# Score runs of two query tiles on four PSUM banks, AV in a transposes' bank, and 256-column units for V, O and the plain FFN

## What is computed

```python
def attn(x, wq, wk, wv, wo):              # 16 heads of 64, window 256, x [16, 2048, 1024] float32
    ...                                   # q, k, v in blocks of 256 tokens, the block before in front of k and v
    scores = jnp.einsum('bhjqd,bhjkd->bhjqk', q, k2) / jnp.sqrt(Dh)
    band = (ki >= qi + 1) & (ki <= qi + W)
    ...
    attn = jax.nn.softmax(jnp.where(mask, scores, neg), axis=-1)
    out = jnp.einsum('bhjqk,bhjkd->bhjqd', attn, v2)
    return out.transpose(0, 2, 3, 1, 4).reshape(B, S, D) @ wo.T

def ffn(x, theta, phi, theta_noise, phi_noise):
    real = x @ jnp.cos(theta + theta_noise)
    imag = x @ jnp.sin(phi + phi_noise)
    return jnp.sqrt(real * real + imag * imag)

x = x + layernorm(attn(layernorm(x), wq, wk, wv, wo))
x = x + layernorm(ffn(layernorm(x), theta, phi, theta_noise, phi_noise))
```

## Time and profile before

| | |
|---|---|
| time, median of 3 runs | 2562.8 us (2562.77 to 2563.14) |
| the profiled execution's own time | 2564.06 us |
| its span, slowest core (2) | 2562.4 us |
| spans of the 8 cores | 2556.4 to 2562.4 us |
| granted clock of TensorE, mean | 0.997 to 0.999 of full speed |
| TensorE busy | 2521.2 us, 98% of the span |
| DVE, ACT, POOL busy | 1400.4 us (55%), 967.4 us (38%), 539.0 us (21%) |

### The profile page before, as it was taken

One profiled execution on the slowest core, in us unless ns is written; L12 is line 12 of the kernel. 1 busy time (PEld: TensorE's weight loads), 2 busy tenths in 40 slices (PEclk: granted clock), 3 DMA queues, 4 the chain that ended last, 5 costly groups with the idle time before them and its releaser, 6 DMA issues.

```text
span 2562.4 us, 47117 instructions; the slowest of 8 cores (2556.4 to 2562.4 us)
## 1 busy us (share of the span) xinstructions
PE 2521.2 (98%) x16752; PEld 1531.6 (60%) x16752; DVE 1400.4 (55%) x2802; ACT 967.4 (38%) x2194; POOL 539.0 (21%) x677
## 2 busy tenths in 40 slices
PE   7999999999999999999999999999999999999998
PEld 6656575758575756656675757575744444444443
DVE  6545454545454546445454545454555466667665
ACT  4424242424242425334342424242535243344333
POOL 0212132222122222212121322221222101111111
PEclk9999999999999999999999999999999999999999
DMA  8211121212221222222222212122273645644563
GB/s 266 67 34 52 49 67 39 62 42 59 42 59 50 50 60 74 67 50 59 58 60 41 67 37 63 42 59 42 75 213 89 193 120 144 156 119 133 139 156 78
DMA packets 261670, 213.50 MB, mean 83 GB/s; under 512 B 178240, under 2 KB 227648, under 8 KB 260416
## 3 DMA queue, kind: packets, MB, share of 16 engines
q1 hardware_dynamic: 261440, 210.49, 31.4%
HBM read 117.64 MB, written 50.33 MB: 66 GB/s over the span
## 4 chain that ended last, share of the span: by engine, by line
PE 94%; DVE 2%; issue 2%; ACT 1%; DMA 1%; SPq 0%; POOL 0%; DVEq 0%; ACTq 0%; POOLq 0%
PE pb L324 23%; PE pb L961 20%; PE pb L365 13%; PE pb L399 13%; PE pb L464 7%; PE pb L541 7%; PE pb L505 6%; PE pb L757 3%; PE pb L621 2%; ACT L484 1%; ACT p_sb L484 0%; DMA r_sb<-thb 0%; DVE pt_sb L514 0%; DVE stats L481 0%; DVE pb L479 0%
## 5 line engine op out<-in xcount | busy, mean ns | idle before, releaser
L324 PE MATMUL pb<-xth,wreg 128*128 128x256 bf16 x3840 | 693.4, 273 | 2.5 <-ACT k_sb L343 1.7
L493 POOL TENSOR_SCALAR p_sb<-p_sb,stats 128x384 f32<-128x384 f32 (+2 forms) x512 | 361.5, 718 | 1258.4 <-DVE stats L489 576.1
L484 ACT ACTIVATE p_sb<-pb,stats 128x384 f32<-128x384 f32 (+2 forms) x512 | 286.2, 560 | 751.7 <-DVE stats L481 727.2
L324 PE MATMUL pb<-xtl,wreg 128*128 128x256 bf16 x1920 | 523.6, 273 | 0.0
L324 PEld LDWEIGHTS pb<-xth,wreg 128*128 128x128 bf16 x3840 | 374.8, 98 | 111.8 <-issue 67.5
L479 DVE TENSOR_TENSOR pb<-pb,mask_s 128x256 f32<-128x256 f32 (+1 forms) x512 | 210.0, 410 | 291.4 <-PE pb L464 291.3
L399 PE MATMUL pb<-wreg,aoh 128*128 128x512 bf16 x1024 | 310.0, 380 | 0.0
L365 PE MATMUL pb<-wreg,xth 128*128 128x512 bf16 x1024 | 305.2, 380 | 3.3 <-DVE v_sb L377 2.4
L481 DVE TENSOR_REDUCE stats<-pb 128x1 f32<-128x384 f32 (+2 forms) x512 | 272.8, 533 | 53.8 <-DVE pb L479 1.4
L514 DVE COPY pt_sb<-pb 128x384 f32<-128x384 f32 (+2 forms) x256 | 135.3, 529 | 211.8 <-PE pb L505 211.0
L464 PE MATMUL pb<-k_sb,q_sb 64*128 64x384 f32 (+2 forms) x1408 | 225.3, 419 | 1.7 <-ACT p_sb L484 1.0
(11 more groups left out here) (115 smaller groups left out, 3146.6 us busy)
## 6 DMA issues: line engine op xcount, KB each, us to landing
x_sb<-x SPq DMA_DIRECT2D x64, 512.0 KB, 5.7
r_sb<-x SPq DMA_DIRECT2D x32, 512.0 KB, 6.6
x<-r_sb SPq DMA_DIRECT2D x32, 512.0 KB, 2.7
wreg<-x SPq DMA_DIRECT2D x32, 512.0 KB, 7.8
y<-wreg SPq DMA_DIRECT2D x64, 256.0 KB, 3.4
trig<-o_sb SPq DMA_DIRECT2D x64, 128.0 KB, 2.1
sums<-o_sb SPq DMA_DIRECT2D x32, 256.0 KB, 4.0
wreg<-trig SPq DMA_DIRECT2D x4, 2048.0 KB, 21.8
```

The costliest lines, as they stand in the source:

```text
L324: e.matmul(bank[b][:, 0:256], a, r, start=s, stop=z)
L484: texp = ac.inc(lambda e, e2=e2, pu=pu, sc=sc: e.activation(pu, sc, AF.Exp, bias=stats[:, col + e2:col + e2 + 1], scale=1.0, accum_out=sta ...
L493: tok["p", e2, qs] = po.inc(lambda e, e2=e2, pu=pu: e.tensor_scalar(pu, pu, stats[:, col + 4 + e2:col + 5 + e2], 1.0, op0=ALU.mult, op1=AL ...
```

## The change

- `unit_steps` is the one form of a dense unit now: 24 matmuls of 256 columns in two halves of 12, in bank 0 or 1 in turn (`small_bank`). V, O and the plain FFN are written in such units, so each of their 512-column matmuls becomes two of 256 columns. `tok_pairs` lists the 24 pairs of a unit with the tokens as the stationary operand. V is evicted by ACT (L372 of the changed kernel) instead of DVE.
- `SB` = 2, 3, 4, 5: the scores of both query tiles stand in one run of a pass, each on two banks of its own. The pass is now: transposes 0, a piece, transposes 1, a piece, both scores, a piece, AV, a piece.
- `TB` = 6, 7 and `AB` = 7: AV writes the bank that head 1's transposes use. Each pair is evicted at once. The first two pairs cannot be written to `aoh` and `aol` while O of the block before reads them; they are put into the part of `k_sb` whose keys are no longer needed, and POOL copies them over at the end of pass 1 (`from_aside`).
- Pass 0 holds O of tile 0 of the block before and half of the second V half, pass 1 the rest of V and O of tile 1. The DMA transposes of x (`xt_rows`) and the load of the next x move from pass 0 to pass 1. In block 0, pass 1 has two halves of V left and nothing behind them, and `xt_fill` stands in pass 1.
- `go` pops `later` before each of the two parts of a piece, so 6 or 7 parts a pass instead of 5.
- Tail: the last O and the plain FFN of block 1 use banks 0 and 1 alone; `wino` uses all 8 banks as before.

```diff
-        DB, SB, TB, AB = (0, 1), (2, 3, 4), (5, 6), 7
+        SB, TB, AB = (2, 3, 4, 5), (6, 7), 7
...
         def dense_bank():
-            b = turn["banks"][turn["d"] % len(turn["banks"])]
+            b = turn["d"] % 8
             turn["d"] += 1
             return b
+
+        def small_bank():
+
+            turn["h"] ^= 1
+            return turn["h"], bank[turn["h"]][:, 0:256]
+
+        def unit_steps(waits, pairs, done):
+
+            st = {}
+
+            def step(half):
+                if half == 0:
+                    st["b"] = small_bank()
+                    pe.wait(*waits(), *bfree[st["b"][0]])
+                key, out = st["b"]
+                t = None
+                for i in range(12 * half, 12 * half + 12):
+                    toks, a, r = pairs[i]
+                    pe.wait(*toks())
+                    f = lambda e, a=a, r=r, i=i: e.matmul(out, a, r, start=(i == 0), stop=(i == 23))
...
+                if half == 1:
+                    bfree[key] = (done(out, t),)
+
+            return [lambda: step(0), lambda: step(1)]
...
+            def done(tt, n4, out, t):
+                o = (g % 2) * 2048 + tt * 1024 + n4 * 256
+                ac.wait(t, tok.get(("av", g - 1, 4 * nh + 3)), *tok.get("wo_st", ()))
+                te = ac.inc(lambda e: e.activation(v_sb[:, o:o + 256], out, AF.Copy))
...
-            sbk = [SB[(turn["s"] + e2) % 3] for e2 in range(2)]
-            turn["s"] += 2
+            sbk = SB[2 * qs:2 * qs + 2]
...
-            b, h0 = AB, (hp % 2) * 256
+            b, h0 = AB, 0
...
+            if hp < 2:
+
+                o = ((g + 1) % 2) * 256
+                cols = slice(hp * 256, (hp + 1) * 256)
+                th, tl = (k_sb[:, m * 512 + o:m * 512 + o + 256].bitcast(BF16)[:, cols] for m in range(2))
+                attend_out(g, th, tl, bank[b][:, 0:256], tok["s", g, 1])
+            else:
+                cols = slice(hp * 256, (hp + 1) * 256)
+                attend_out(g, aoh[:, cols], aol[:, cols], bank[b][:, 0:256], tok.get(("o_pe", g - 1)))
...
+        def from_aside(g):
+            o = ((g + 1) % 2) * 256
+            po.wait(*tok["ao", g], tok.get(("o_pe", g - 1)))
+            for m, dst in enumerate((aoh, aol)):
+                src = k_sb[:, m * 512 + o:m * 512 + o + 256].bitcast(BF16)
+                tok["aside", g] = po.inc(lambda e, dst=dst, src=src: e.tensor_copy(dst[:, 0:512], src))
...
-                    n = (5 if s < 5 else 6) if g == 0 else (7 if s in (2, 6) else 6)
+                    n = 7 if s in (2, 6) else 6
...
                 def go(n):
-                    if later:
-                        later.pop(0)()
+                    for k in (n - n // 2, n // 2):
+                        if later and (k or not n):
+                            later.pop(0)()
+                        run(dense, k)
+                        n = 1
+
+                n = len(dense)
+                transposes(g, s, 0)
+                go(n // 4)
...
                 transposes(g, s, 1)
-                go(per[2])
...
+                go((n + 1) // 4)
...
+                if s < 7 or not last:
+                    for qs in range(2):
+                        scores(*((g, s + 1) if s < 7 else (g + 1, 0)), qs)
+                go((n + 2) // 4)
+                if s == 1 and g > 0:
+                    xt_rows(0, [tok["v", g, 1], tok["v_pe"]])
+                attend(g, s)
+                go((n + 3) // 4)
                 if s == 1:
-
-                    evict()
-
-                if s == 0:
+                    from_aside(g)
+
+                if s == 1:
```

More of the change, by code:

```diff
@@ L307, in kq_steps, with kq_out @@
         def kq_steps(g, m, which):
[L309 to L335, removed]
+            pairs = []
+            for kc in range(KC):
+                xh, xl = (v[:, kc * 256:(kc + 1) * 256] for v in (xth, xtl))
+                pairs += [(lambda kc=kc: tok["xt", 0, kc // 2], a, r) for a, r in three(
+                    wh(which, kc, m * 128, 128), wl(which, kc, m * 128, 128), xh, xl)]
+            return unit_steps(lambda: tok["w", which], pairs, lambda out, t: kq_out(g, m, which, out, t))
+        def kq_out(g, m, which, src, t):
+            ac.wait(t, tok.get(("s", g - 1, m)), tok.get(("aside", g - 1)) if which == 0 and m < 2 else None)
             if which == 0:
@@ new lines, in o_steps, with done @@
+        def o_steps(g, tt):
+            def done(n4, out, t):
+                tok["o_pe", g] = t
+                ac.wait(t, tok.get("o_free"))
+                te = ac.inc(lambda e: e.activation(o_sb[:, n4 * 256:(n4 + 1) * 256], out, AF.Copy))
+                if n4 == 3:
+                    later.extend(ln_o(g, tt, te))
+                return te
+            steps = []
+            for n4 in range(4):
+                steps += unit_steps(lambda: (*tok["w", 3], *tok["ao", g], tok["aside", g]),
+                                    tok_pairs(aoh, aol, 3, tt, n4, lambda kc: ()),
+                                    lambda out, t, n4=n4: done(n4, out, t))
+            return steps
@@ L777, in f_steps, with done @@
-            return [lambda k=k: step(k) for k in range(3)]
+            def done(n4, out, t):
+                o = tt * 1024 + n4 * 256
+                dst = (sq if r == 0 else mg)[:, o:o + 256]
+                tok["f_pe", b % 2] = t
+                ac.wait(t, tok.get(("mg", tt, nh)))
+                te = ac.inc(lambda e: e.activation(dst, out, AF.Square))
+                if r == 1 and n4 % 2 == 1:
+                    o = tt * 1024 + nh * 512
+                    later.extend(ln_m(b, tt, nh, nh == 1, mg[:, o:o + 512], sq[:, o:o + 512], te))
+                return te
@@ L1208, in build_nc @@
             later.pop(0)()
-        turn["banks"] = DB + SB[:2]
         tok["wino", 0] = tok["wino", 1] = tok["o_pe", NB - 1]
@@ L1218, in build_nc @@
                 later.pop(0)()
-        turn["banks"] = tuple(range(8))
         for b in range(2, NB):
```

200 lines of the change are left out of this document (55 added, 145 removed).

## The result

The changed kernel takes **2650.8, 2653.4, 2670.9 and 2680.2 us** in four runs, against 2562.8 to 2563.1 us before: ratio **1.039, 95% interval 1.031 to 1.048**, so slower by 3.9%.

What follows compares the result with a forecast made beforehand. TensorE's own instructions were taken to set the time. Merged runs -11.4, splitting +9.0, waits gone -11, queue waits +81, parts without rows +21, clock +10 make +98.6 us on 2562.8: 2660 us, range 2615 to 2700.

Steps and rivals of the forecast that it cites:

- The queues behind the score run: Steady blocks: second mask and four Exps delay evictions and copies, 6.2 us of waits per block, +81 us over 13 blocks.
- The 2.2: Pass 6, LayerNorm of x: AV's evictions come late, so the next transposes in AV's bank wait 2.2 us.
- Splitting: V, O and plain FFN: 3456 matmuls of 512 columns become two of 256 each, +9.0 us.
- the waits that go: TensorE's idle time before AV (7.8 us) and V (3.3 us) vanishes: -11 us, bounds 0 and -15.
- The merged score run: One score run for both tiles saves one entry of 0.09 us in each of 127 passes: -11.4 us.
- Block 15 and the tail: Two banks for units of 2.6 us, with square roots on ACT: +8 us (-3 to 20).
- The clock: One in four of 26 new waits of about 2 us lowers TensorE's clock, costing 1.5 us each: +10 (0 to 40).
- My plain block: A steady block gets new waits of 3 x 0.33 + 1.93 + 1.08 + 2.2 = 6.2 us.
- The rival "queues keep up": ACT's evictions behind the Exps come in time, only TensorE's count matters: 2549 us; chance of faster 0.12.

Runs made afterwards that it cites:

- e11_wide_apart2: `e7_wide` with the two score runs apart by one dense step that draws its side work: 2588.4 and 2591.1 us on cores 0 and 1.
- the mended order: The changed kernel with masks first, LayerNorm behind pass 7 and sines spread over passes 3 to 5 together: 2553.0 and 2554.4 us.
- e3_masks: The changed kernel, with VectorE issuing masks and maxima of both query tiles' four score banks before the reciprocals: 2581.5 us, ratio 1.0076.
- e7_wide: The changed kernel with masks first, LayerNorm behind pass 7, sines spread, and V, O, plain FFN back in 512-column units: 2544.5 us, ratio 0.9931.

## Why the prediction was right, point by point

The time of 2660 us lies inside the interval, 7 to 9 us above the two lowest times of the changed kernel, and the mechanism is the one named. Two terms were far off, in opposite directions, so that the total came this near is partly luck: the merged runs saved 27 us more than I had, block 15 and the tail cost 18 more, and the other blocks and the clock make up the rest.

**The queues behind the score run: right.** Second mask at 4.12 us (predicted 4.12), ACT free at 6.89 (6.98), waits of 0.41 three times (0.33), 2.00 (1.93), 1.25 (1.08), 1.80 (2.2), together 6.3 (6.2) per block. Releasers and places are those predicted. Moving the LayerNorm and the sines away took exactly the wait put down to each; masks first took the three of 0.41 and the one of 1.25, and parts of the other two. The 2.2 was 1.8 since ACT began the high part of x 532.36 - 531.39 = 0.97 us behind DVE's start, where I let 8.8 - 7.18 = 1.6 pass.

**Splitting, and the waits that go: right.** 2.6 ns per split matmul, seen three times. The idle time before AV and V fell from 11 to under 1 us.

**The merged score run: -11.4 predicted, about -38 measured.** This is the step that failed. I took the 0.85 us of one run as work that doubles, and gave the merging the entry of 0.09 alone. A merged run lasts 497.94 - 496.45 = 1.49 us in the rows above, not 1.70. So 0.21 us of each 0.85 are also a cost of entering and leaving, which I had excluded with the words "without an exit cost". The starts of the single matmuls in after show where it lies. They go in pairs, one of each head: at 496.45, 496.88, 497.20 and 497.52, and the next dense one at 497.94. So the first pair takes 0.43 us, an inner one 0.32 and the last 0.42. The rows that I had read of before show only runs of two pairs, a first and a last. But its trace has 96 longer ones, of narrower matmuls, and there the answer stood: in 48 of them the pairs start at 0, 0.32, 0.54 and 0.65 us and the run ends at 0.86, so of the two pairs of 256 columns the first takes 0.32 and the inner one 0.22, and of the two of 128 columns the inner one takes 0.11 and the last 0.21. 127 x (0.09 + 0.21) = 38; `e11_wide_apart2` gives 0.305 per pass.

**Block 15 and the tail: +8 (-3 to 20) predicted, 25.8 net measured,** outside my bounds. TensorE's waits there sum up to 21.9 us on core 3, and to 3.3 before. The chain of work that ended last on core 3, in block 15:

```profile
2032.13 0.90 PE pb L449 x4
...
2038.37 0.68 ACT p_sb L469 x2
2039.10 0.40 issue
2039.59 0.67 DVE wreg L761
...
2041.62 0.63 ACT wreg L763
2042.52 0.28 ACT wreg L742
2042.80 0.39 ACT pt_sb L496
2043.20 0.52 PE pb L490 x3
```

From the scores to the transposes not one step is TensorE's: masks, Exp of both tiles one behind the other, then the plain FFN's sum (L761), the load of the square root's table (1.28 us, at 2040.33) and the root (L763), the eviction, the copy: 11 us, in which TensorE has no more dense work than in other passes. I had the steady passes' queue in hand and did not work it out for this block, where the square root stands ahead of the copy. The tail has one wait more, on TensorE, DVE and ACT of core 3:

```profile
2107.96 1.44 PE L171 MATMUL pb<-wreg,q_sb 128*128 128x256 bf16 x6 [6.65 <-ACT wreg L742]
```

```profile
2103.78 0.69 DVE L835 TENSOR_TENSOR r_sb<-x_sb 128x512 f32<-128x512 f32 x1 [8.60 <-DMA x<-r_sb]
```

```profile
2107.45 0.36 ACT L742 ACTIVATE wreg<-pb 128x256 f32<-128x256 f32 x1
```

DVE stands 8.6 us until a store from `r_sb` to x is done, the square root waits for DVE, the eviction (L742) stands behind the square root and a high part of 1.04 us, and TensorE waits 6.65 us for it. Whether more banks would have taken this wait away in the changed kernel isn't shown.

**The clock: +10 for the steady waits predicted, found elsewhere.** On core 3 the granted clock stays at 1.00 at all waits of about 2 us in steady blocks (the longest, in block 13, is 2.18), as in the first stretch below. Between the start and the last microseconds it is at the lower of its two levels (1.2 of 2.4 GHz) for 27 us, in six places: in block 0, in each of the two blocks with two sine chunks, and three times in block 15 and the tail. Five of these lie at one wait of 2.59 us or more by the profile's figures (2.67 in block 7, 3.65 before the second stretch below). In block 0 it fell behind four waits of 1.69 us and less that lie close together, while in block 15 two waits of 1.90 and 1.49 us, 3.3 us apart, went without a fall. I can't give a rule: core 1 has a fall at the very wait of 2.18 us at which core 3 has none, and before the change core 2 had one at 1.58. The 0.76 below is a mean of the two levels. Two stretches of core 3 (length, busy of the engines, clock, DMA):

```profile
494.00:500.00 6.00, 5.63 (x45) 4.32 (x46) 4.20 (x8) 2.29 (x5) 0.00 (x0) 1.00 0.32 90
```

```profile
2041.00:2048.00 7.00, 4.80 (x29) 4.10 (x30) 2.14 (x4) 3.04 (x7) 0.26 (x1) 0.76 0.53 134
```

The mean clock went from 0.998 to 0.993. Over the span that is at most 0.005 x 2648 = 13 us (an estimate: a part of it fell on time in which TensorE waited anyway). I have not separated the two. So a term of 10 us may be of the right size, but for waits other than those that I named.

**By region, core 3,** from the first transposes of each block: start and block 0 +4.7, blocks 1 to 6 and 9 to 13 +42.0 (3.8 each), blocks 7 and 14 +14.6, block 8 -0.3, block 15 and tail +25.8; together the 86.8. My plain block would have been 6.2 + 0.5 - 0.7 - 0.7 = 5.3 us longer, 58 in eleven of them and so 16 too many; for all else I had 98.6 - 58 = 40, where 45 were measured.

**The rival "queues keep up" (2549 us)** lies near what the mended order reaches with the change's own units, 2553.0 us, but by luck. With 38 us for the merged runs in place of 11.4 its sum would be 2522, and the waits of blocks 0, 7, 14 and 15, of which the three edits left 29 us on core 3, are not in it. Its condition, the second tile's mask well before 4.1 us, is what masks-first makes (it comes at 486.89 - 483.82 = 3.07 us in `e3_masks`); alone that was not enough, as waits of 1.6 and 0.9 us stayed.

## What to carry to other kernels

When two short runs become one, put everything on TensorE's side of the sum that a run costs at both its ends (look for a longer run in the same trace before you scale a short one), and ask each in-order queue behind it what now stands twice in front of the next eviction; a step that waits (here the reciprocals) in the middle of a queue is the one to move behind the others. A gain can be real and hidden: here 38 us lay under 120 us of waits on core 3, and three edits of the order that touch no operation brought 98 of them back. An edit that also changes how side work is drawn tests two things; hold one still.

## What the runs showed of the hardware

- A run of 64-row fp32 matmuls of 384 columns between 128-row bf16 ones costs some 0.3 us for being entered and left: four take 0.85 us, eight in one run 1.49. It is 0.09 before the first start, and 0.11 and 0.10 in the first and the last pair (0.43 and 0.42 us, where an inner pair takes 0.32). `e11_wide_apart2` against `e7_wide` gives 0.305 us per pass.
- Two matmuls of 256 columns take 2.6 ns more than one of 512 (2 x 109.4 against 216.2), whether in O alone (+0.23 us per 96) or in V and O (+0.48 per 192).
- On core 3 of the changed kernel, single waits of up to 2.18 us did not lower the granted clock; at each of those of 2.59 us or more it was at its lower level for some microseconds (a mean of 0.76 over 7 us in block 15), and once behind four shorter waits. Core 1 had a fall at the wait of 2.18 us.
